# Graph network, edge MLP: the second layer's bias moves from a TensorE matmul to a VectorE add out of PSUM

## The reference

```python
edge_input = jnp.concatenate([x[row], x[col], edge_attr, d_raw], axis=-1)
h = jax.nn.silu(edge_input @ ew1 + eb1)
m_ij = jax.nn.silu(h @ ew2 + eb2)
agg = jax.ops.segment_sum(m_ij, row, num_segments=x.shape[0])
node_in = jnp.concatenate([x, agg], axis=-1)
upd = jax.nn.silu(node_in @ nw1 + nb1) @ nw2 + nb2
```

## Time and profile before

| | |
|---|---|
| median of 3 runs | 9372.87 us (9367.48 to 9378.12) |
| profiled execution, its own time | 9370.1 us |
| its span, first to last instruction | 9368.2 us |
| TensorE busy in the span | 7249.4 us, 77% |
| VectorE | 6071.2 us, 65% |
| ScalarE | 4885.8 us, 52% |
| GpSimd | 6324.9 us, 68% |
| TensorE's mean granted clock | 0.707 of 2.4 GHz |

### The profile page before, as it was taken

How to read it: one execution, slowest core, us unless ns; L and a number is a source line. 1 busy time by engine, 2 the same in 40 slices (tenths; PEclk the granted TensorE clock), 3 DMA queues, 4 the chain that set the end, 5 groups by cost and what they waited for, 6 DMA issues and landing times.

```text
span 9368.2 us, 235997 instructions
## 1 busy us (share of the span) xinstructions
PE 7249.4 (77%) x52596; PEld 5744.2 (61%) x52823; DVE 6071.2 (65%) x27239; ACT 4885.8 (52%) x11854; POOL 6324.9 (68%) x7563
## 2 busy tenths in 40 slices
PE   2466666666689999998699999999966777777776
PEld 2355555555578888887366666666645555555554
DVE  7777732222233343343799999999976777777776
ACT  4122233333334444443467667777736777777775
POOL 0377777777766666663577777777737777777775
PEclk9988888888899999999555555555555555555555
DMA  4122222222222222221222222222241111111114
GB/s 142 43 54 55 54 59 60 59 61 60 60 75 70 70 72 70 71 71 33 54 55 54 55 54 55 54 55 54 55 33 29 28 28 28 28 28 28 28 28 27
DMA packets 990523, 491.42 MB, mean 52 GB/s; under 512 B 830665, under 2 KB 841468, under 8 KB 990140
## 3 DMA queue, kind: packets, MB, share of 16 engines
q0 software_dynamic: 168832, 302.29, 14.8%
q1 hardware_dynamic: 701756, 169.41, 9.8%
q10 hardware_dynamic: 119840, 18.68, 1.2%
HBM read 356.46 MB, written 151.48 MB: 54 GB/s over the span
## 4 chain that ended last, share of the span: by engine, by line
PE 26%; issue 23%; POOL 23%; DVE 17%; DMA 6%; DVEq 2%; ACT 1%; POOLq 1%; SPq 0%; ACTq 0%
POOL z_s L640 18%; DMA arena<-table,arena 5%; POOL arena L690 5%; PE ps_all L965 5%; PE ps_all L975 4%; PE ps_all L992 4%; PE ps_all L1100 3%; PE ps_all L989 3%; DVE shift L1531 2%; DVE arena L1535 2%; DVE arena L1490 2%; PE ps_all L1076 1%; DVE arena L1576 1%; PE ps_all L1001 1%; PE ps_all L977 1%
## 5 line engine op out<-in xcount | busy, mean ns | idle before, releaser
L690 POOL DMA_INDIRECT arena<-table,arena x3616 | 3471.1, 960 | 1500.5 <-issue 984.6
L640 POOL DMA_INDIRECT z_s<-arena x1660 | 1755.0, 1057 | 853.1 <-issue 504.5
L1100 PE MATMUL ps_all<-arena 128*128 128x132 f32 (+1 forms) x7232 | 1809.1, 429 | 1.8 <-DVE acc L1593 1.8
L1100 PEld LDWEIGHTS ps_all<-arena 128*128 128x128 f32 x7232 | 1606.4, 325 | 2.6 <-issue 2.6
L829 ACT ACTIVATE arena<-lanes_b,arena 128x128 bf16<-128x128 bf16 x3616 | 1147.1, 387 | 415.6 <-DVE arena L1464 407.1
L1490 DVE TENSOR_REDUCE arena<-ps_all 128x2 f32<-128x1024 f32 x904 | 1098.2, 1215 | 18.3 <-PE ps_all L1117 18.3
L1117 PE MATMUL ps_all<-arena,pick 28*128 28x512 bf16 (+1 forms) x2260 | 1081.7, 597 | 0.5 <-DVE arena L1490 0.5
L1076 PE MATMUL ps_all<-ident_b,arena 128*128 128x128 bf16 x3616 | 541.0, 303 | 645.1 <-DMA arena<-table,arena 434.0
L745 ACT ACTIVATE arena<-ps_all 18x512 f32<-18x512 f32 x415 | 243.2, 586 | 1381.0 <-PE ps_all L952 1367.2
L1386 DVE TENSOR_TENSOR arena<-lanes,arena 128x512 f32<-128x512 f32 x452 | 322.8, 714 | 973.8 <-PE ps_all L965 973.8
L853 ACT ACTIVATE arena<-ps_all 28x512 bf16<-28x512 bf16 (+1 forms) x904 | 522.6, 578 | 717.2 <-PE ps_all L1076 717.2
(11 more groups left out here) (260 smaller groups left out, 16454.3 us busy)
## 6 DMA issues: line engine op xcount, KB each, us to landing
arena<-z_s SPq DMA_DIRECT2D x452, 264.0 KB, 2.7
arena<-table,arena POOLq DMA_INDIRECT x3616
arena<-rec_d SPq DMA_DIRECT2D x1660, 10.0 KB
z_s<-arena POOLq DMA_INDIRECT x1660
rec_d<-in_rec ACTq DMA_DIRECT2D x1, 16160.0 KB, 58.4
arena<-ids_d SPq DMA_DIRECT2D x904, 4.0 KB
arena<-pos_d ACTq DMA_DIRECT2D x830, 0.5 KB
arena<-pos_d SPq DMA_DIRECT2D x830, 0.5 KB
```

The costliest lines, as they stand in the source:

```text
L640: pool.indirect_dma_start(z_s, bass.IndirectOffsetOnAxis(ap=slot[:, g.slot(SLOTS), u:u + 1], axis=0), z_out[:, g.slot(SLOTS), u, :], None) ...
L690: pool.indirect_dma_start(g_rows[:, r, u * step + CODE_WORDS:(u + 1) * step], None, tables[n], bass.IndirectOffsetOnAxis(ap=ids[:, r, 0, u ...
L1100: mm = pe.matmul(ps[6][:, 0:out_w], a_hot_f[:, g.slot(4), u, :], g_msg[:, g.slot(4), u * out_w:(u + 1) * out_w], start=(u == 0), stop=(u = ...
```

## The change

The bias matmul goes, and with it `ones_b`, `b_rows` and the five operations that split the bias into bf16 parts. The bias is loaded into all 128 partitions of `b_mid` by one broadcast DMA. VectorE adds it on the way out of PSUM (`of(3)`, first in its step) and writes `msg`, which now has four buffers; ScalarE's Silu works on `msg` in SBUF, in place, after the new semaphore `biased`. TensorE's sum over the messages comes one step later (`of(5)`), and VectorE's L1375 too (`of(6)`), so the pipeline is one step deeper. `hot_f` gets eight buffers in place of four.

```diff
-        b_mid = sb("b_mid", [1, F_HID])
+        b_mid = sb("b_mid", [P, F_HID])
-        hot_f, at = carve(at, [4, U, P])
+        hot_f, at = carve(at, [SLOTS, U, P])
-        msg, at = carve(at, [2, U, F_HID])
+        msg, at = carve(at, [4, U, F_HID])
...
-            sp.wait_ge(S("b_part_ready"), 1)
-            sp.dma_start(b_rows[0:3, :], b_part.rearrange("a k f -> a (k f)")).then_inc(S("rows_in"), 16)
+            sp.wait_ge(S("w_dist_ready"), 1)
             sp.dma_start(w_edge[KX - 2:KX - 1, :], w_dist).then_inc(S("rows_in"), 16)
...
-            pool.memset(b_rows, 0.0).then_inc(S("weights_clear"), 1)
...
             def edge_mlp(of):
                 g = of(3)
                 if g is not None:
-                    act.wait_ge(S("hidden2"), g.done())
-                    if g.back(2).exists():
-                        act.wait_ge(S("summed"), g.back(2).done())
-                    act.activation(msg[:, g.slot(2)].rearrange("p u f -> p (u f)"), ps[4 + g.slot(2)], ACT.Silu
-                                   ).then_inc(S("message_ready"), 1)
+                    act.wait_ge(S("biased"), g.done())
+                    act.activation(msg[:, g.slot(4)], msg[:, g.slot(4)], ACT.Silu).then_inc(S("message_ready"), 1)
...
             def edge_mlp(of):
-                g = of(4)
+                g = of(5)
...
-                        mm = pe.matmul(ps[6 + r][:, 0:F_HID], hot_f[:, g.slot(4), u, :], msg[:, r, u, :],
+                        mm = pe.matmul(ps[6 + r][:, 0:F_HID], hot_f[:, g.slot(SLOTS), u, :], msg[:, g.slot(4), u, :],
...
                     pe.wait_ge(S("mid_ready"), g.done())
                     if g.back(2).exists():
-                        pe.wait_ge(S("message_ready"), g.back(2).done())
+                        pe.wait_ge(S("biased"), g.back(2).done())
                     for u in range(U):
-                        pe.matmul(ps[4 + r][:, u * P:(u + 1) * P], mid_e[:, r, u * P:(u + 1) * P], w_mid,
-                                  start=(u == 0), stop=False, skip_group_check=True)
-                    mm = pe.matmul(ps[4 + r].rearrange("p (u f) -> p u f", u=U), ones_b,
-                                   b_rows.unsqueeze(1).broadcast_to([P, U, F_HID]), start=False, stop=True,
-                                   skip_group_check=True)
+                        mm = pe.matmul(ps[4 + r][:, u * P:(u + 1) * P], mid_e[:, r, u * P:(u + 1) * P], w_mid, start=True, stop=True)
                     mm.then_inc(S("hidden2"), 1)
...
             link(dve.tensor_scalar(w_dist, w_dist, 1.0 / CUTOFF, None, ALU.mult))
-            link(dve.tensor_copy(b_part[:, 0, :], b_mid))
-            link(dve.tensor_tensor(b_rest, b_mid, b_part[:, 0, :], ALU.subtract))
-            link(dve.tensor_copy(b_part[:, 1, :], b_rest))
-            link(dve.tensor_tensor(b_rest, b_rest, b_part[:, 1, :], ALU.subtract))
-            link(dve.tensor_copy(b_part[:, 2, :], b_rest))
-            dve.sem_inc(S("b_part_ready"), 1)
+            dve.sem_inc(S("w_dist_ready"), 1)
...
             def edge_mlp(of):
-                g = of(5)
+                g = of(3)
+                if g is not None:
+                    dve.wait_ge(S("hidden2"), g.done())
+                    if g.back(4).exists():
+                        dve.wait_ge(S("summed"), g.back(4).done())
+                    dve.tensor_tensor(msg[:, g.slot(4)], ps[4 + g.slot(2)].rearrange("p (u f) -> p u f", u=U),
+                                      b_mid.unsqueeze(1).broadcast_to([P, U, F_HID]), ALU.add).then_inc(S("biased"), 1)
+                g = of(6)
...
-                    if g.back(4).exists():
-                        dve.wait_ge(S("summed"), g.back(4).done())
-                    dve.tensor_tensor(hot_f[:, g.slot(4)], lanes.unsqueeze(1).broadcast_to([P, U, P]), lane, ALU.is_equal
+                    if g.back(SLOTS).exists():
+                        dve.wait_ge(S("summed"), g.back(SLOTS).done())
+                    dve.tensor_tensor(hot_f[:, g.slot(SLOTS)], lanes.unsqueeze(1).broadcast_to([P, U, P]), lane, ALU.is_equal
                                       ).then_inc(S("hot_ready"), 1)
```

More of the change, by code:

```diff
@@ L221, in gnn_kernel @@
         ones = sb("ones", [P, P])
-        ones_b = sb("ones_b", [P, P], BF16)
         zero = sb("zero", [P, 1])
@@ L228, in gnn_kernel @@
         w_mid = sb("w_mid", [F_HID, F_HID])
-        b_mid = sb("b_mid", [1, F_HID])
-        b_rest = sb("b_rest", [1, F_HID])
-        b_part = sb("b_part", [1, 3, F_HID], BF16)
-        b_rows = sb("b_rows", [P, F_HID], BF16)
+        b_mid = sb("b_mid", [P, F_HID])
         w_node_h = sb("w_node_h", [F_IN, F_HID])
@@ L407, in _ @@
                     sp.dma_start(to[:, part_cols(k)], edges_of(ends, k).rearrange("(p j) -> p j", p=P)).then_inc(S(name), 16)
-            sp.wait_ge(S("weights_clear"), 2)
+            sp.wait_ge(S("weights_clear"), 1)
             loads = [
@@ L413, in _ @@
                 (w_edge[KX - 1:KX, :], eb1.rearrange("(a n) -> a n", a=1)),
-                (w_mid, ew2), (b_mid, eb2.rearrange("(a n) -> a n", a=1)),
+                (w_mid, ew2), (b_mid, eb2.rearrange("(a n) -> a n", a=1).broadcast_to([P, F_HID])),
                 (w_node_h, nw1[0:F_IN, :]), (w_node_a, nw1[F_IN:, :]), (w_out, nw2),
@@ L921, in _ @@
                       ).then_inc(S("tables_shown"), 1)
-            pe.wait_ge(S("rows_in"), 32)
+            pe.wait_ge(S("rows_in"), 16)
             pe.wait_ge(S("chunks_ready"), 1)
@@ L1002, in edge_mlp @@
                     mm.then_inc(S("hot_turned"), 1)
-            edge_pipeline(pe, GROUPS, 4, edge_mlp)
+            edge_pipeline(pe, GROUPS, 5, edge_mlp)
             pe.wait_ge(S("mlp_done"), 1)
@@ L1151, in _ @@
             link(dve.tensor_scalar(lane_rest, lane_col, -1.0, float(P), ALU.mult, ALU.add))
-            link(dve.memset(ones_b, 1.0))
             link(dve.memset(lane_code, 0.0))
@@ L1383, in edge_mlp @@
                                       ).then_inc(S("hot_ready"), 1)
-                    if g.back(4).exists():
-                        dve.wait_ge(S("summed"), g.back(4).done())
-                    dve.tensor_tensor(hot_f[:, g.slot(4)], lanes.unsqueeze(1).broadcast_to([P, U, P]), lane, ALU.is_equal
+                    if g.back(SLOTS).exists():
+                        dve.wait_ge(S("summed"), g.back(SLOTS).done())
+                    dve.tensor_tensor(hot_f[:, g.slot(SLOTS)], lanes.unsqueeze(1).broadcast_to([P, U, P]), lane, ALU.is_equal
                                       ).then_inc(S("hot_ready"), 1)
             src_buckets = Rounds(dve, mybir.EngineType.DVE, src_bucket, NT - 1, SLOTS, 2 * SLOTS)
-            edge_pipeline(dve, GROUPS, 5, edge_mlp, src_buckets.load)
+            edge_pipeline(dve, GROUPS, 6, edge_mlp, src_buckets.load)
             dve.wait_ge(S("added"), GROUPS)
```

## The result

The changed kernel takes 9431.85 us, median of 4 runs (9429.94 to 9433.90), against 9371.12 for the kernel before on the same chip (4 runs, 9367.48 to 9378.12). The ratio is 1.0065, 95% interval 1.0049 to 1.0081: slower by 61 us where 100 us less was forecast, and above the range.

What follows compares the result with a forecast made beforehand. The prediction took TensorE's issue in the edge MLP, 3.82 us a group, as the bound. Bias matmul -99.4, setup -1.3 and drain +0.5 summed to -100.2 us, from median 9372.9 to 9273 us, range 9262 to 9325.

Steps and rivals of the forecast that it cites:

- TensorE as the bound: Edge MLP: TensorE stays the bound at 3.60 us a group, 9265 to 9282 us in all, chance 0.72.
- L977 at 0.22: Edge MLP: the bias matmul holds TensorE for 0.22 us a group, 452 times, so removing it saves 99.4 us.
- The add at 0.70 us: Edge MLP: the new bias add on VectorE takes 0.70 us a group, bounds 0.69 and 0.86.
- L778's margin of 0.19 us: Edge MLP, ScalarE: the message's Silu is out of the way 0.19 us before the first layer's Silu can start.
- the whole cushion of 0.41: Edge MLP: the add may be 0.41 us slower than taken before TensorE loses anything.
- GpSimd unhurt: Edge MLP: the add's effect on GpSimd is priced at nothing, since casts beside L1375 all last 0.29 us.
- rival D: Edge MLP: the add holds GpSimd, which becomes the bound at 3.74 to 3.90 us a group, 9337 to 9409 us, chance 0.10.
- Rivals B: Edge MLP: VectorE starts each round of eight groups late, costing 13 to 68 us, 9286 to 9341 us, chance 0.07.
- C: Edge MLP: the chain add, Silu, L778 is late in every group, 9285 to 9360 us, chance 0.07.
- Rival E: Edge MLP: weight loads or issue limit TensorE first, only 0.13 of 0.22 us comes back, 9314 us, chance 0.04.
- The setup: Ahead of the chunk stage: five chained operations go, so that stage starts 1.3 us earlier.
- The numbers: Closing part with range 9262 to 9325 us and chances faster 0.91, same 0.05, slower 0.04; untouched attention layers keep their time.

Runs made afterwards that it cites:

- before_no_bias: Kernel before with the bias matmul L977 left out, VectorE's program unchanged: 12359.68 us, 0.9922 of the kernel before on a slower chip.
- after_add2_pad59: Changed kernel with the bias add done twice, first into a scratch tile, and 59 empty VectorE instructions: 9290.44 us, 0.9939 of the kernel before.
- after_pad79: Changed kernel with 79 empty VectorE instructions in the node update: 9246.95 us, 0.9894 of the kernel before on a third chip.
- after_headslot: Changed kernel without a pad, VectorE's attention loops asking the compiler for a fixed start place: 9244.55 us, 0.9891 of the kernel before.
- before_pad17_b: Kernel before with 17 empty VectorE instructions in the node update, on a second chip: 9540.72 us, 1.0163 of the kernel before.
- before_pad128: Kernel before with 128 empty VectorE instructions in the node update: 9384.75 us, 0.9997 of the kernel before.
- before_pad17: Kernel before with 17 empty VectorE instructions ahead of the node update, on the slower chip: 12450.00 us, 1.000 of the kernel before.
- before_pad5: Kernel before with 5 empty VectorE instructions in the node update: 9487.62 us, 1.0150 of the kernel before on a third chip.
- after_again: The changed kernel itself, run again on a second chip: 9446.29 us, 1.0060 of the kernel before.
- after_pad111: Changed kernel with 111 empty VectorE instructions in the node update: 9452.30 us, 1.0072 of the kernel before.
- after_pad96: Changed kernel with 96 empty VectorE instructions ahead of the node update: 12379.06 us, 0.9944 of the kernel before on the slower chip.

## Why the prediction was wrong

**Right, with its sizes.** TensorE as the bound, at 3.60 us a group (3.603). L977 at 0.22 (0.2155 by before_no_bias, 97.5 / 451 = 0.216 here). The add at 0.70 us (0.691, all of 452 within 690 to 692). The Silu from SBUF at 0.61 (0.630, inside its bounds). The wait of the add for L966, 1.5 us a group (651.4 / 430 = 1.51). L778's margin of 0.19 us (0.18); the whole cushion of 0.41 was 0.1 too small, and a second path of the same width was missing (after_add2_pad59), which cost nothing here. GpSimd unhurt: it waits 0.96 us a group for TensorE (408.8 / 425), where it waited 0.70, so rival D fell; all 425 of its casts that overlap the add last 0.29, as the 53 pairs said. A cast that overlaps L1374, a one-hot with both inputs in SBUF, lasts 0.47 to 0.57 in all but one of 425 cases, so that one-hot does slow GpSimd, within its slack. Rivals B and C fell as well: TensorE is idle 1.9 us in 1550. Rival E fell: the whole slot came back. The setup starts the chunk stage 1.7 us earlier (340.9 against 342.6) for 1.3 forecast.

**The step that failed** is the one under "The numbers": "the attention layers, untouched and at 0.51 from 6000 us on the earlier trace rows, should keep their time, and half of the span hangs on that". In the sum it is a term of 0 with no reason but "untouched". Their source is untouched, their place in VectorE's program isn't: it moved by 37 instructions, the loops came to lie across four pieces instead of three, and each round fetches five packets again (278 in layer 1, where it had 13). Layer 1 took 160.2 us more; with the loops in place (after_pad79, after_headslot) the same edge MLP gives 0.9894 and 0.9891, and the place alone, without the change (before_pad17_b), gives 1.0163. Those two shares, times 9371, are -99 and +153 us, together +54; 61 was measured. The prediction does say that a different length of the attention stage would be outside all of its rivals, and that is what came.

**Why the share is so different in the two layers.** Both are fetched after. In layer 1 VectorE is busy 2236.27 of 2480 us, and what it loses at a round's start, 208.4 - 75.9 = 132.5 us at L1504 alone, nobody gives back. In layer 2 it is busy 1612.06 of 2400, 67%; the same line is idle 227.5 us there where it was 86.1, and the layer is 1.7 us longer (7 in before_pad17_b, 2304.1 against 2297.0 in before_pad128): the wait took the place of others. What the layer waits for is the gathers: TensorE waits 397.4 us at one line for gathered rows after, and 394.9 before. On the chip of 12456 us layer 1 is like that too, and before_pad17 costs nothing there (1.000). A fetched layer 1 costs 135 us in before_pad5 (2506.5 - 2371.7, same chip) and 160 to 172 in the others (after 160.2, before_pad17_b 160.3, after_again 166.9, after_pad111 172.3, each less 2394.3), with as many packets. The stall behind the branch is the same: the fourth instruction of a round starts 3.00 us behind it in before_pad5 and 0.38 in after_pad79 on that chip, 2.92 and 0.30 in after and before; 2.62 us in 53 rounds are 139 us. The other 0.4 us a round in the dearer ones comes later in the round; whether the chip or the loop's place makes it isn't known.

**What could have been seen.** The page of before has the row that carries it, `q14 instruction: 64, 0.52, 0.0%`, which I read as nothing. After it is:

```profile
q14 instruction: 594, 4.87, 0.2%
```

0.2% of the DMA engines' time is nothing indeed; what counts is who waits behind it. And with the instructions counted, a loop of 356 that must stay within 384 has by the rule 29 places in 128 at which it is kept, so that 3 in 4 shifts would lose it. I counted every instruction of the change by what it costs to execute, and none by how far it moves the code behind it.

The Trainium skill (Runtime: NRT & Kernel Launch, Instruction fetch mechanics) says that a branch taken to a target outside the window of loaded pages stalls until the page is fetched, which is the shape of the stall here. By its sizes, two pages of 16 KiB, the places would have to be counted modulo 256 and be at most 156 (512 - 356); for before to be kept and before_pad5 not, before would be at 152 to 155 or so, and after_pad96, 133 on, at about 30, where it is kept. It is fetched. The packets here are of 8 KB and the limit fits at three of them, so for VectorE the measurement decides. (Four pieces of 8 KB, the three and one ahead, are as much as those two pages together; that the difference lies only in how the store is divided is a guess that no run tests.)

## What to carry to other kernels

When an edit makes a stage faster by its own profile and the program slower, compare stage by stage and look in the untouched ones for idle time that ends by "issue" at the start of a loop's rounds, beside the packets of the instruction queue. A loop body of VectorE whose length comes near three pieces (here 356 of 384 instructions) is kept or lost by a shift of a few instructions anywhere ahead of it on the same engine, waits included; give its head a fixed place before judging an edit (here the ratio is 0.9891 with it, and 1.0060 and 1.0065 without on two other chips). An estimate from the rule: a body of up to 257 instructions (384 - 127) is kept at any place, and one over 384 at none; no run here has loops of those lengths at the edge. A loop that is fetched anew costs much only where that engine is what the loop waits for.

## What the runs showed that I had not expected

- A loop of 356 instructions of VectorE is fetched anew in each round, five packets of 8192 bytes, at one place and never at another; 5 instructions without work moved the time by 1.5%, 17 by 1.6%, 128 by nothing (0.9997).
- The round's start then idles 3.97 us where it idled 1.40.
- Waits are instructions: the edge MLP's loop grew from 54 to 77 on VectorE, by eight adds, one a group, and fifteen instructions for waits and registers.
- Layer 1 hides or shows this by the chip: 3721 us with it and 3750 without (before_pad17, before_no_bias, with the same code in the layer) on a chip with slower gathers, 2555 against 2394 on another (before_pad17_b, before_pad128).
